# A two-layer graph kernel: the element-wise factor work of the start moves from GpSimd to VectorE, ScalarE makes its high parts ahead of the scores, and x is loaded in eight transfers

## The reference

```
h, W, a1, a2: Wh = x @ W                       # x: 8192 x 128, adj: 8192 x 8192 (int32, sparse, symmetric)
e  = (Wh @ a1)[:, None] + (Wh @ a2)[None, :];  e = where(e > 0, e, 0.2 * e);  e = where(adj > 0, e, -9e15)
x  = layernorm(x + elu(softmax(e, axis=1) @ Wh))                        # layer 0
x1 = adj @ x / rowsum(adj)
x  = layernorm(x + concat([x1, x]) @ weight + bias)                     # layer 1
```

## Time and profile before

| | |
|---|---|
| time, median of 3 runs (lowest, highest) | 1636.6 us (1633.95, 1637.88) |
| time of the profiled execution | 1634.6 us |
| its span, first to last instruction | 1632.8 us |
| busy share of the span | PE 96%, ACT 61%, DVE 54%, POOL 29% |
| first matmul of group 0 (L718) | 66.07 us |
| first matmul of group 1 | 121.5 us |
| PE idle before L718, up to 125 us, for DVE L942 | 27.5 us in 4 waits |

### The profile page before, as it was taken

One profiled execution on the slowest core, in us unless ns is written; L12 is line 12 of the kernel. 1 busy time (PEld: TensorE's weight loads), 2 busy tenths in 40 slices (PEclk: granted clock), 3 DMA queues, 4 the chain that ended last, 5 costly groups with the idle time before them and its releaser, 6 DMA issues.

```text
span 1632.8 us, 46669 instructions
## 1 busy us (share of the span) xinstructions
PE 1562.7 (96%) x16966; PEld 1375.6 (84%) x16966; DVE 889.4 (54%) x3323; ACT 1003.1 (61%) x2513; POOL 479.3 (29%) x583
## 2 busy tenths in 40 slices
PE   7379999999999999999999999998999999999998
PEld 6268888888888888888888888887888888888887
DVE  6885555555555565555555555554445454454443
ACT  3768999899989989998999899982000010000100
POOL 0654433443443344334433443440000000000000
PEclk9589999999999999999999999999999999999999
DMA  8537787778777777777777777743000000000000
GB/s 266 194 129 272 274 283 280 271 278 280 285 272 276 280 278 270 281 271 272 273 280 284 273 276 283 284 163 86 20 16 16 16 17 19 16 16 16 19 16 16
DMA packets 100859, 302.82 MB, mean 185 GB/s; under 512 B 5856, under 2 KB 68064, under 8 KB 68064
## 3 DMA queue, kind: packets, MB, share of 16 engines
q1 hardware_dynamic: 100832, 302.48, 51.9%
HBM read 289.77 MB, written 12.68 MB: 185 GB/s over the span
## 4 chain that ended last, share of the span: by engine, by line
PE 92%; issue 1%; DVE 0%; ACT 0%; POOL 0%; DVEq 0%; POOLq 0%
PE acc L718 55%; PE acc L780 28%; PE pack_ps L682 6%; PE turn_ps L804 2%; PE turn_ps L794 1%; DVE factors L942 0%; POOL one L388 0%; ACT level_ring L619 0%; DVE stats L971 0%; DVE row_sums L1016 0%; DVE rows_y L1034 0%; ACT part_sums L613 0%; DVE rows_y L983 0%; DVE row_sums L1021 0%; DVE mv L978 0%
## 5 line engine op out<-in xcount | busy, mean ns | idle before, releaser
L508 ACT ACTIVATE level_ring<-s_row,cols 128x256 fp8e4<-128x256 f32 x2048 | 839.3, 498 | 4.9 <-DMA s_row<-s_and_t 4.9
L718 PE MATMUL acc<-factors,edge_ring 128*128 128x258 f16 x4096 | 544.5, 274 | 35.2 <-DVE factors L942 27.5
L718 PE MATMUL acc<-factors,level_ring 128*128 128x258 f16 x4096 | 543.5, 274 | 0.0
L780 PE MATMUL acc<-factors,adj_ring 128*128 128x258 f16 x4096 | 470.5, 274 | 5.0 <-issue 5.0
L718 PEld LDWEIGHTS acc<-factors,edge_ring 128*128 128x128 fp8e4 x4096 | 392.1, 98 | 94.6 <-DVE factors L942 27.8
L780 PEld LDWEIGHTS acc<-factors,adj_ring 128*128 128x128 fp8e4 x4096 | 400.4, 98 | 64.1 <-issue 5.2
L718 PEld LDWEIGHTS acc<-factors,level_ring 128*128 128x128 fp8e4 x4096 | 400.9, 98 | 60.4
L928 DVE TENSOR_TENSOR level_ring<-level_ring,edge_ring 128x1024 uint16<-128x1024 uint16 x256 | 187.8, 735 | 239.2 <-ACT level_ring L508 231.4
L935 DVE TENSOR_TENSOR edge_ring<-edge_ring,level_ring 128x1024 uint16<-128x1024 uint16 x256 | 195.9, 796 | 0.0
L611 ACT ACTIVATE part_sums<-acc 128x258 f32<-128x258 f32 x32 | 12.4, 386 | 298.1 <-PE acc L780 298.1
L386 POOL TENSOR_SCALAR one<-mv 128x2 f32<-128x2 f32 x64 | 24.7, 386 | 552.6 <-DVE mv L978 552.6
(11 more groups left out here) (102 smaller groups left out, 861.4 us busy)
## 6 DMA issues: line engine op xcount, KB each, us to landing
adj_ring<-in_adj SPq DMA_DIRECT2D x128, 2048.0 KB, 7.7
x_parts<-parts SPq DMA_DIRECT2D x32, 129.0 KB, 4.7
factors<-x_parts SPq DMA_DIRECT2D x8, 516.0 KB, 3.9
factors<-in_x SPq DMA_DIRECT2D x16, 256.0 KB, 3.3
s_row<-s_and_t SPq DMA_DIRECT2D x32, 128.0 KB, 4.6
rows_x<-in_x SPq DMA_DIRECT2D x32, 128.0 KB, 4.3
x_rows<-rows_y SPq DMA_DIRECT2D x32, 128.0 KB, 7.8
rows_x<-x_rows SPq DMA_DIRECT2D x32, 128.0 KB, 2.1
```

What stands on the lines that cost most here:

```text
L508: a = act.activation(level_bytes[:, h % MASK_SLOTS, j, :, :], s_halves[:, slot, :, :], ACT.Relu, bias=t_big[:, h * HALF + j:h * HALF + j + ...
L718: m = pe.matmul(acc[a][:, 0:ROW], mask, factors[:, neg, jj, :], start=(jj == 0), stop=(jj == NJ - 1))
L780: m = pe.matmul(acc[b][:, 0:ROW], ring_1_bytes[:, c, j, b, :], factors[:, 0, jj, :], start=(jj == 0), stop=(jj == NJ - 1))
```

## The change

DVE now makes all eight products (`make_product`) and all eight low parts (`low_of`); POOL makes none. On DVE a unit is: two low parts, the two products of the next unit, then the unit's masks. ACT makes the two high parts of a unit ahead of its scores. The small DVE operations of the start are put in another order: `e_col` and `f_col` are scaled at once, the first two products follow, and the denominator columns and what `u_col`, `v_col` need come behind them. The largest of the last Wh tile is taken behind the largest and smallest t. x has a place of its own in SBUF for all 16 tiles, and is loaded in eight transfers of 512 KB that wait for nothing; two 2 MB pieces of `adj` follow on the same queue. The loops over x tiles are written out on all engines, and piece 0 of `adj` is packed before the last tile's Wh rather than before the last four.

```diff
-            for k in range(X_SLOTS):
-                sp.dma_start(x_in[:, k], x_tiles[:, XB * k:XB * (k + 1), :]).then_inc(x_in_sem[k], 16)
+            for k in range(NX // 2):
+                sp.dma_start(x_in[:, 2 * k:2 * k + 2].rearrange("p k j f -> p (k j) f"),
+                             x_tiles[:, 2 * XB * k:2 * XB * (k + 1), :]).then_inc(x_in_sem[k], 16)
             load_adj(0, 0)
-            with sp.Fori(1, NX // X_SLOTS) as n:
-                for k in range(X_SLOTS):
-                    sp.wait_ge(x_turned, X_SLOTS * (n - 1) + k + 1)
...
-            pool.wait_ge(ef_ok, 2)
-            make_product(0)
-            for c in range(UPG):
-                make_product(2 * c + 1)
-                if c < UPG - 1:
-                    make_product(2 * c + 2)
-                low_of_f(c)
...
-            act.wait_ge(s_row_in[0], 16)
             for c in range(UPG):
-                for h in (2 * c, 2 * c + 1):
-                    scores(0, 0, h, True)
                 for k in range(2):
                     act.wait_ge(product_ok, 2 * c + k + 1)
                     act.activation(factors[:, k, c * UNIT:(c + 1) * UNIT, 0:F], product[:, (2 * c + k) % 3, :, :],
                                    ACT.Copy)\
                         .then_inc(high_ok, 1)
+                if c == 0:
+                    act.wait_ge(s_row_in[0], 16)
+                for h in (2 * c, 2 * c + 1):
+                    scores(0, 0, h, True)
...
+            turn_x(0)
+            for k in range(NX):
+                if k + 1 < NX:
+                    turn_x(k + 1)
+                make_wh(k)
+                if k == NX - 2:
+                    pe.wait_ge(pack_w_ok, 1)
+                    packable(0, 0, first=True)
+                    pack(0)
...
+            def make_product(n):
+
+                c, k = n // 2, n % 2
+                js = slice(c * UNIT, (c + 1) * UNIT)
+                if n < 3:
+                    dve.wait_ge(ef_ok, k + 1)
+                else:
+                    dve.wait_ge((e_low_ok, f_low_ok)[(n - 3) % 2], (n - 3) // 2 + 1)
+                dve.tensor_tensor(product[:, n % 3, :, :], wh[:, js, :],
+                                  (e_col, f_col)[k][:, js].unsqueeze(2).to_broadcast([P, UNIT, F]), ALU.mult)\
+                    .then_inc(product_ok, 1)
...
+            def low_of(n, done):
+
+                c, k = n // 2, n % 2
                 js = slice(c * UNIT, (c + 1) * UNIT)
-                dve.wait_ge(high_ok, 2 * c + 1)
...
+                dve.wait_ge(high_ok, n + 1)
+                dve.tensor_tensor(factors[:, k, js, FD:FD + F], product[:, n % 3, :, :], factors[:, k, js, 0:F],
+                                  ALU.subtract)\
+                    .then_inc(done, 1)
...
             for c in range(UPG):
+                low_of(2 * c, e_low_ok)
+                low_of(2 * c + 1, f_low_ok)
+                if c < UPG - 1:
+                    make_product(2 * c + 2)
+                    make_product(2 * c + 3)
                 masks(0, c)
-                low_of_e(c)
```

More of the change, by code:

```diff
@@ L129, in adj_resnorm_kernel @@
         product = early_of["product"].rearrange("p (k j f) -> p k j f", k=3, f=F)
[L130 to L131 removed]
+        x_in = factors[:, 1, :, :].rearrange("p j r -> p (j r)").bitcast(F32)[:, 0:NJ * F]\
+            .rearrange("p (k j f) -> p k j f", k=NX, f=F)
         x_t = product[:, 2, 0:2 * XB, :].rearrange("p (k j) f -> p k (j f)", k=2)
@@ L146, in adj_resnorm_kernel @@
         consts_in, w0_in, a0_in, w1_in, bias_in = (sem(n) for n in "consts_in w0_in a0_in w1_in bias_in".split())
-        x_in_sem = [sem(f"x_in{k}") for k in range(X_SLOTS)]
+        x_in_sem = [sem(f"x_in{k}") for k in range(NX // 2)]
         adj_in = [sem("adj_in0"), sem("adj_in1")]
@@ L468, in _, with copy_turned @@
             act.activation(wq[:, F:F + 2], turn_ps[1][:, 0:2], ACT.Copy).then_inc(wa_ok, 1)
[L470 to L477, removed]
+            def copy_turned(k):
+                act.wait_ge(x_turned, k + 1)
+                if k >= 2:
+                    act.wait_ge(wh_made, k - 1)
+                act.activation(x_t[:, k % 2, :], turn_ps[k % 2][:, :], ACT.Copy, accum_out=x_sums[:, k:k + 1])\
+                    .then_inc(x_t_ok, 1)
             def copy_words(g, c):
@@ L483, in copy_words @@
                     .then_inc(words_ok, 1)
-            copy_turned(0, True)
-            with act.Fori(1, NX // 2) as n:
-                copy_turned(n)
+            copy_turned(0)
+            for k in range(1, NX):
+                copy_turned(k)
             act.wait_ge(s_turned, 1)
@@ L576, in _ @@
                         .then_inc(high_ok, 1)
+                if c == 0:
+                    act.wait_ge(s_row_in[0], 16)
+                for h in (2 * c, 2 * c + 1):
+                    scores(0, 0, h, True)
+                if c == 0:
+                    act.wait_ge(uy_ok, 2)
+                    act.activation(u_col, uy_col, ACT.Exp).then_inc(exp_cols_ok, 1)
+                    act.activation(v_col, vy_col, ACT.Exp).then_inc(exp_cols_ok, 1)
                 next_words(0, c)
@@ L639, in _, with turn_x @@
             pe.wait_ge(ones_ok, 1)
[L641 to L645, removed]
+            def turn_x(k):
+                if k % 2 == 0:
+                    pe.wait_ge(x_in_sem[k // 2], 16)
+                if k >= 2:
+                    pe.wait_ge(x_t_ok, k - 1)
                 for j in range(XB):
@@ L648, in turn_x, with make_wh @@
                 m.then_inc(x_turned, 1)
[L650 to L654, removed]
+            def make_wh(k):
+                pe.wait_ge(x_t_ok, k + 1)
+                if k >= 2:
+                    pe.wait_ge(wh_ok, k - 1)
                 for j in range(XB):
@@ L659, in make_wh @@
                 m.then_inc(wh_made, 1)
[L661 to L668, removed]
             def packable(g, c, first=False):
@@ L831, in _, with copy_wh, largest_wh @@
             dve.memset(parts[:, :, ROW - 1:ROW], 0.0).then_inc(tail_ok, 1)
-            def copy_wh(n, k):
-                dve.wait_ge(wh_made, 2 * n + k + 1)
+            def copy_wh(k):
+                dve.wait_ge(wh_made, k + 1)
+                j0 = XB * k
                 for half in range(2):
[L836 to L839, removed]
+                    bank = acc[2 * (k % 2) + half][:, 0:2 * (F + 2)].rearrange("p (j f) -> p j f", j=2)
+                    dve.tensor_copy(wh[:, j0 + 2 * half:j0 + 2 * half + 2, :], bank[:, :, 0:F])
+                    d = dve.tensor_copy(cols[:, 0:2, j0 + 2 * half:j0 + 2 * half + 2],
+                                        bank[:, :, F:F + 2].rearrange("p j k -> p k j"))
                 d.then_inc(wh_ok, 1)
-                dve.wait_ge(wh_ok, 2 * n + k + 1)
-                dve.tensor_reduce(wh_top[:, bass.ds(2 * n + k, 1)], wh[:, bass.ds(2 * XB * n + XB * k, XB), :], AX.XY,
+            def largest_wh(k):
+                dve.wait_ge(wh_ok, k + 1)
+                dve.tensor_reduce(wh_top[:, k:k + 1], wh[:, XB * k:XB * (k + 1), :], AX.XY,
                                   ALU.max, apply_absolute_value=True).then_inc(top_ok, 1)
-            with dve.Fori(0, NX // 2) as n:
-                for k in range(2):
-                    copy_wh(n, k)
+            for k in range(NX):
+                copy_wh(k)
+                if k < NX - 1:
+                    largest_wh(k)
+            dve.wait_ge(wh_ok, NX)
             dve.tensor_reduce(top_low[:, 0:1], t_col, AX.X, ALU.max).then_inc(t_top_ok, 1)
             dve.tensor_reduce(top_low[:, 1:2], t_col, AX.X, ALU.min).then_inc(low_ok, 1)
+            largest_wh(NX - 1)
             dve.wait_ge(low_ok, 1)
```

42 lines of the change are left out of this document (12 added, 30 removed).

## The result

| | before | changed kernel |
|---|---|---|
| median | 1635.28 us | 1608.24 us (1606.3 to 1611.39, 4 runs) |
| ratio | | 0.9836, 95% interval 0.9813 to 0.9858 |
| time and span of the profiled execution | 1634.6, 1632.8 us | 1608.12, 1606.3 us |
| first matmul of group 0, of group 1 | 66.07, 121.5 us | 54.52, 95.5 us |

The changed kernel is 27 us (1.6%) faster; forecast were 1614 us, 22 us faster, and a range from 1610. The same kernel run again with the second set of experiments gave 1610.16 us (1608.6 to 1612.1), ratio 0.9851, 0.9836 to 0.9866. The direction and the place were right.

The account below looks back on a forecast made before the run. PE was taken as the bound, held up in group 0 by DVE's low parts, late because of POOL. Group 1 at 99.3 plus 1511.3 gave 1610.6 us span, plus 1.8 and 2.0: 1614.4, rounded 1614; range 1610 to 1620.

Parts of the forecast that it names:

- The register work of the loops: DVE's loops over x tiles at the start: writing them out saves register work priced at nothing.
- the unit after a wait: PE in group 0: a unit with its packing takes 9.75 us after a wait, partly at low clock.
- the step to the median: End of the sum: the profiled execution lay 2.0 us under the median, so 1612.4 became 1614.4 us.
- What bounds, and that the rest is carried over: PE's chain bounds; from group 1 to the end 1511.3 us stay unchanged, so only group 1's start counts.
- The price of an operation: DVE in group 0: a product costs 2.2 us, like its nearest row L942; a low part 2.28 us.
- Group 0 step by step: First product at 38.8 us, first masks at 56.7, 69.1, 81.5, 89.5; group 1 at 99.3 instead of 121.5.
- Products dear on DVE: Rival, group 0: products cost POOL's 3.9 us on DVE, giving 1628 us; chance 0.07.
- POOL's silent stretch moving to its next operation: Rival: POOL's silent 7.41 us delays group 0's softmax, so masks come late: 1618 to 1621 us; chance 0.08.
- Gain given back: Rival: ACT starts group 1 further behind, PE waits in each group: 1632 to 1637 us, no change; chance 0.04.
- DVE the bound by far: Rival, group 0: products and low parts both cost POOL's price on DVE, giving 1645 us; chance 0.04.
- 2.5 from x: Start: x queued ahead of adj removes DVE's idle 2.66 us, a gain of 2.5 us, between 1.7 and 2.9.

Follow-up runs that it names:

- products_twice: Changed kernel with each of the eight products made twice on DVE, the second waiting for the first; 1626.84 us (0.9959).
- loops_out: Kernel before with only the four loops over x tiles written out, x still loaded through four slots; 1634.41 us (0.9999).
- act_scores_first: Changed kernel with ACT's order undone: scores ahead of the high parts, as before; 1616.78 us (0.9899).
- after_again: The changed kernel run once more, unchanged; 1610.16 us.
- wh_copies_shared: Changed kernel with ACT copying the first PSUM bank of each x tile (Wh and score columns), DVE the second; 1607.22 us (0.9838).
- no_x: Changed kernel with x transfers undone (four slots, looped loading, as before); loops over x tiles stay written out; 1616.50 us (0.9890).
- low_f_on_pool: Changed kernel with the low parts of f given back to POOL, all else kept; 1618.46 us (0.9903).

## Why the prediction fell short, and what of it was right

The forecast was 1614 us and its lowest value 1610; measured were 1608.24. What bounds, which waits go and in what order the units come was right. The step that failed is the sizing of three terms of the sum. The register work of the loops, priced at nothing, was 1.4 us over the x tiles; the unit after a wait, taken as 9.75 us, took 8.02 in the first profile; and the step to the median, taken as 2.0 us, was 0.1 there.

*What bounds, and that the rest is carried over.* Right: 1510.8 us from group 1 to the end in both executions of the changed kernel, against 1511.33 before. The traces of the other kernels, which change nothing there either, lie between 1507.7 (products_twice) and 1511.6 (loops_out), so carrying it over is good to a few us and no better.

*The price of an operation.* Right: 2.29 us a product by itself, 4.49 for two in a row, as its nearest row L942 had it; products_twice gives 2.3 on the path.

*Group 0 step by step.* From the first product to the first mask's use: forecast 17.9, measured 17.6, with the moved small operations at 1.0 us instead of 1.6 and the large ones at 2.25 to 2.3 instead of 2.2. From unit 0 to unit 2: forecast 24.8, measured 24.9. ACT's parts were never late in group 0, and act_scores_first shows what hid them.

*Three terms were mis-sized*, and together they are 5.7 of the 6.2 us between 1614.4 and 1608.24:

1. "Written-out loops save register work that I price at nothing: the pace is that of DVE's own operations." The pace went from 1.61 to 1.52 us a tile, also in loops_out where nothing else changed. Over the 15 steps from the first tile to the last that is 1.4 of the 1.6 us by which the copies ended earlier than forecast (33.63 against 35.2). The operations between the copies and the first product were 0.3 us shorter, and the way from there to the masks another 0.3: 2.1 us in all at unit 2.
2. The low clock in unit 2: I took 9.75 us for a unit after a wait, as in the earlier trace rows; it took 8.02 at full clock. That is 1.7 us. In after_again, after the same wait, it took 10.7. So no single value is right here: behind a wait of 2.69 us the unit took 8.02 us in three executions (the first profile, act_scores_first, wh_copies_shared) and 10.7 in two (after_again, no_x). That the span of after_again, 1610.3, lies on the forecast 1610.6 is luck: its unit 2 was 1.0 us slower than forecast, and its start 0.7 us and its rest 0.5 us shorter.
3. The step from the profiled execution to the median: I added 2.0 us, the distance to a median of three runs. With more runs the median before is 1635.25, 0.65 over the profiled time, and the profiled time of the changed kernel lies on its median. That made 1.9 us, and it stood in the forecast as if it were known.

The remaining 0.5 us lie behind the start of group 1. None of these alone would have left the range. The prediction names margins of 0.8, 1, 1.7 and 1.5 us, for x, the small operations, the clock and the median's spread. Added up they reach from 1614.4 down to 1609.4, and the range stopped at 1610. The register work was in none of them, and the step to the median only as that spread. With the second set's 1610.16 the time would have been just inside; the terms were mis-sized all the same.

*Rivals.* Products dear on DVE: no (2.29 us). POOL's silent stretch moving to its next operation: no; POOL's first tensor operation at 96.33 waited for DVE alone, the softmax that follows kept the distances it had, and low_f_on_pool shows the stretch lying ahead of the release of the operation. The load of about 6 us that the Trainium skill names ("GPSIMD Engine Reference", section "Instruction dispatch") is somewhat shorter than the stretch (6.87 to 8.32 us in three kernels); that the two are the same isn't shown. By that rule, the prediction said, this rival would be the case; here it isn't, for the stretch is over before the next operation comes. Gain given back: no. DVE the bound by far: no, though products_twice shows the slope on which it would lie.

*The split of the gain.* By medians x is worth 4.5 us alone (its trace shows 1.45 of them at the first product) and 6 to 8 in the changed kernel, and 4.9 between two profiles with an equally slow unit 2; whether it is worth more in the changed kernel isn't shown. ACT's order is worth 6.6 to 8.5. The remaining 14 (1630.71 to 1616.78) are the move of the products and low parts from POOL, with the new order of the small DVE operations, which no run separates. The prediction's "2.5 from x" was too small by the 1.4 us of the loops and because the wait for x that it removes is 2.7 to 5 us, not a fixed 2.66.

## What to carry to other kernels

Find the engine whose list sets each stage's start, and count instructions on it one to one; an operation moved onto that list can still pay if it ends a mutual blockade with POOL and a slower price there. When you move a producer to another engine's list, look at who must answer before that list goes on (here ACT's high parts), and put that answer first. Waits read from a single profile are one draw, and so is the time of a unit behind a short wait (8.0 or 10.7 us here). Before you carry one into a forecast, give it the spread that neighbouring runs show, and don't add the distance to a median of three as if it were a cost.

## What was not expected of the hardware

- After the same wait of 2.69 us PE's unit with its packing ran once at a mean clock of 1.00 (8.02 us) and once at 0.73 (10.72 us), in two executions of the same kernel. Three more kernels show both values: 8.02 twice and 10.7 once.
- A loop with register-addressed operations cost DVE 0.09 us a tile over five operations (1.61 against 1.52 us).
- POOL's silent stretch behind the all-reduce (6.87 to 8.32 us) runs while POOL waits for the input of its next operation: in low_f_on_pool that operation began 0.61 us after its input was ready.
- The wait for an x transfer queued behind 2 MB of adj was 2.66, 4.24 and 4.95 us in three executions with the same order of transfers (before, loops_out, no_x); the first Wh copy with x up front came at 9.95 and at 11.25 us.
